# A selective-scan kernel: in each POOL step, the due inflows ahead of the C product of the last chunk

## What is computed

```python
def _ssm(u, Wdbc, Wdt, bdt, Alog, Dp):          # u: (batch, time, 1024)
    dlt, Bm, Cm = split(einsum('bse,re->bsr', u, Wdbc))
    delta = softplus(einsum('bsr,er->bse', dlt, Wdt) + bdt)
    dA = exp(delta[..., None] * -exp(Alog))      # 16 states n
    dBu = delta[..., None] * Bm[:, :, None, :] * u[..., None]
    h_t = dA_t * h_(t-1) + dBu_t                 # a scan over time, per state
    y_t = einsum('ben,bn->be', h_t, C_t)         # sum over the 16 states
    return y + u * Dp
act_mx = silu(einsum('bsd,ed->bse', x_ssm, Wx) + bx)
out = einsum('bse,de->bsd', act_mx * (z1 + z2), Wf) + bf + skip   # z1 forward, z2 backward
return x + gate * out
```

## Time and profile before

| | |
|---|---|
| median of three runs | 3446.78 us |
| range of the three | 3441.18 to 3452.31 us |
| the profiled execution: its time, its span | 3441.2 us, 3439.6 us |
| VectorE (DVE) busy | 3141.1 us, 91% of the span |
| POOL busy | 3134.4 us, 91% |
| TensorE (PE) busy | 2896.7 us, 84% |
| ScalarE (ACT) busy | 2628.9 us, 76% |
| mean granted TensorE clock | 0.933 of full speed |
| unit 20, an mx unit, from its first scan to the next unit's | 1249.35 to 1296.41, 47.1 us |

### The profile page before, as it was taken

One profiled execution on the slowest core, in us unless ns is written; L12 is line 12 of the kernel. 1 busy time (PEld: TensorE's weight loads), 2 busy tenths in 40 slices (PEclk: granted clock), 3 DMA queues, 4 the chain that ended last, 5 costly groups with the idle time before them and its releaser, 6 DMA issues.

```text
span 3439.6 us, 47915 instructions
## 1 busy us (share of the span) xinstructions
PE 2896.7 (84%) x16208; PEld 2088.2 (61%) x16208; DVE 3141.1 (91%) x2117; ACT 2628.9 (76%) x5032; POOL 3134.4 (91%) x1418
## 2 busy tenths in 40 slices
PE   8997788887778888888889888888889888888888
PEld 4654565666656665566666665666666665666665
DVE  1865999999999999999999999999999999999994
ACT  0225899887887899887777899987777898987772
POOL 0534999999999999999999999999999999999996
PEclk9998999999889999999999999999999999998999
DMA  5566443654456444644557344645557444644553
GB/s 208 199 219 230 148 154 132 221 194 160 148 193 245 133 154 158 246 152 165 186 196 258 131 157 152 250 151 165 182 202 255 131 160 152 246 154 163 183 194 120
DMA packets 224041, 623.12 MB, mean 181 GB/s; under 512 B 21980, under 2 KB 68252, under 8 KB 219960
## 3 DMA queue, kind: packets, MB, share of 16 engines
q1 hardware_dynamic: 221064, 599.11, 50.2%
q0 software_dynamic: 2592, 18.88, 1.6%
q10 hardware_dynamic: 144, 2.10, 0.2%
HBM read 539.75 MB, written 80.24 MB: 180 GB/s over the span
## 4 chain that ended last, share of the span: by engine, by line
POOL 33%; issue 23%; PE 21%; DVE 13%; ACT 1%; DMA 0%; POOLq 0%; DVEq 0%; SPq 0%; ACTq 0%
POOL dbu L1075 17%; POOL hbuf L1080 15%; DVE hbuf L1179 7%; PE y L797 7%; PE mb L770 6%; DVE slot L1179 4%; PE slot L808 3%; PE mb L844 1%; DVE du L1130 1%; PE mb L847 1%; DVE delta L1120 1%; PE mb L880 1%; PE slot L880 0%; PE y L880 0%; POOL skip L1086 0%
## 5 line engine op out<-in xcount | busy, mean ns | idle before, releaser
L1080 POOL TENSOR_TENSOR hbuf<-hbuf,cres 128x1024 f32<-128x1024 f32 x640 | 1508.1, 2373 | 33.6 <-DVE hbuf L1179 32.6
L1075 POOL TENSOR_TENSOR dbu<-bst,du 128x1024 f32<-128x1024 f32 x640 | 1506.9, 2373 | 34.5 <-DVE du L1130 22.5
L797 PE MATMUL y<-ident,hbuf 128*128 128x128 f32 x8192 | 1129.0, 289 | 295.3 <-POOL hbuf L1080 292.1
L797 PEld LDWEIGHTS y<-ident,hbuf 128*128 128x128 f32 x8192 | 997.2, 149 | 486.2 <-POOL hbuf L1080 384.7
L1001 ACT ACTIVATE abuf<-dut,bt 128x128 f32<-128x128 f32 x3072 | 971.0, 387 | 0.0
L1179 DVE TENSOR_TENSOR_SCAN hbuf<-dec,slot 128x1024 f32<-128x1024 f32 x384 | 874.6, 2278 | 41.8 <-PE slot L808 23.7
L1179 DVE TENSOR_TENSOR_SCAN slot<-slot,dbu 128x1024 f32<-128x1024 f32 x384 | 875.6, 2280 | 10.7 <-ACT slot L1039 5.3
L1039 ACT ACTIVATE slot<-delta,par 128x1024 f32<-128x1024 f32 x640 | 710.3, 1110 | 211.9 <-DVE hbuf L1184 198.5
L1179 DVE TENSOR_TENSOR_SCAN hbuf<-slot,dbu 128x1024 f32<-128x1024 f32 x256 | 580.5, 2268 | 1.7 <-ACT slot L1039 1.7
L808 PE MATMUL slot<-ident,abuf 128*128 128x128 f32 x3072 | 424.5, 283 | 178.7 <-ACT abuf L1001 170.7
L1039 ACT ACTIVATE dec<-delta,par 128x1024 f32<-128x1024 f32 x384 | 438.2, 1141 | 156.7 <-DVE hbuf L1179 156.7
(11 more groups left out here) (140 smaller groups left out, 2142.7 us busy)
## 6 DMA issues: line engine op xcount, KB each, us to landing
bst<-bc_s SPq DMA_DIRECT2D x640, 512.0 KB, 4.2
cres<-bc_s SPq DMA_DIRECT2D x128, 512.0 KB, 8.2
wzs<-wz_s SPq DMA_DIRECT2D x64, 256.0 KB
yf_s<-yrd SPq DMA_DIRECT2D x32, 512.0 KB, 5.4
ybuf<-yf_s SPq DMA_DIRECT2D x32, 512.0 KB, 5.8
yg_s<-ybuf SPq DMA_DIRECT2D x31, 512.0 KB, 2.9
si_s<-silu SPq DMA_DIRECT2D x28, 512.0 KB, 6.0
silu<-si_s SPq DMA_DIRECT2D x28, 512.0 KB, 4.5
```

The costliest lines, as they stand in the source:

```text
L797: last = nc.tensor.matmul(y[:, j * P:(j + 1) * P], hbuf[:, q % HR, j * P:(j + 1) * P], ident[:], start=False, stop=(q % N == N - 1), is_tr ...
L1075: nc.gpsimd.tensor_tensor(dbu[:, i % DR, :], bst[:, i % BR, :], du[:, k % 2, :], ALU.mult).then_inc(pool_b, 1)
L1080: nc.gpsimd.tensor_tensor(hbuf[:, q % HR, :], hbuf[:, q % HR, :], cres[:, q % N, :], ALU.mult).then_inc(pool_prod, 1)
```

## The change

```diff
             for k in range(NU):
                 for c in range(N):
                     q = N * k + c
+                    for i in INFLOWS_AT[q]:
+                        inflow(i)
                     if q >= 1 and kind(q - 1) != "V":
                         product(q - 1)
-                    for i in INFLOWS_AT[q]:
-                        inflow(i)
                     if c == 3 and k > 0 and projection_of(k - 1) is not None:
                         finish_result(projection_of(k - 1))
```

## The result

| | before | after |
|---|---|---|
| median of four runs each on one chip | 3449.55 us | 3506.82 us |
| lowest to highest | 3441.18 to 3455.54 | 3495.47 to 3518.60 |
| profiled execution, its span | 3441.2, 3439.6 | 3511.82, 3510.2 |
| mean granted clock in it | 0.933 | 0.939 |

The ratio is 1.0172, with a 95% interval of 1.0146 to 1.0198: the change costs 59 us, 50 to 68. The forecast was 3512.5 us in a range of 3470 to 3565, and slower.

What follows compares the result with a forecast made beforehand. VectorE and POOL, both 91% busy without slack, were taken as the bound. Terms 41.6 + 22.1 - 10 + 12 = 65.7 us, added to a median of 3446.8, gave 3512.5 us, range 3470 to 3565.

Steps and rivals of the forecast that it cites:

- TensorE's new wait: Step 14, mx units: TensorE waits about 2.45 us for the later product of chunk 13 before its sum.
- stall, 32 mx boundaries: Behind step 14 of mx units: VectorE starts the next unit's scan 2 1.3 us later, 32 times, 41.6 us.
- low clock: TensorE behind its wait in mx boundaries: clock falls in 13 of 32, 1.7 us each, 22.1 us.
- absorbed: VectorE's waits for TensorE's turned inflow swallow part of the stall: -10 us, between 0 and 23.7.
- gating units: Step 14, 30 boundaries: POOL's earlier inflow waits 0.4 us for `du`, delaying the next scan 2; 12 us.
- steps 2 and 8: Products of chunks 1 and 7 go behind inflows of chunks 5 and 13; claimed to cost nothing.
- The walk: Step 14, mx units: late product 13 delays its sum, last Wx part, sigmoid, decay and scan 2, by 1.3 us.
- The strict reading: TensorE's clock drops only after an idle monitor window, so short waits cost no clock; the 22.1 us would go.
- rival A: Full clock: TensorE's new wait never costs the clock; +43.6 us, 3490.4 us, chance 0.27.
- Rival C: Absorbed: the stall at scan 2 replaces later waits of VectorE and ScalarE; about +5 us, 3452 us, chance 0.08.
- the wait of L797 at the sum of chunk 13: Sign on TensorE: its wait for POOL moves here from the sum of chunk 14, about 2.4 us in mx units.
- The new waits of L976: Sign on ScalarE: the sigmoid waits about 1.8 us for the last Wx part, some 60 us over 32 boundaries.

Runs made afterwards that it cites:

- the kernel with the decay first: The changed kernel, with ScalarE's decay of chunk 2 put ahead of the second sigmoid half; 3510.10 us, 1.0202.
- one inflow ahead: The kernel before, with only the first of step 14's two inflows ahead of the product of chunk 13; 3456.86 us, 1.0036.
- product 4 ahead: The kernel before, with the product of chunk 4 put ahead of the inflow of chunk 9; 3438.82 us, 0.9980.
- the same with Wf later: The kernel before, product of chunk 4 ahead of inflow of chunk 9, and unit 8's Wf load moved from step 0 to 3; 3429.41 us, 0.9958.
- gating units alone: The kernel before, with the product of chunk 4 ahead of the inflow of chunk 9 only in gating units; 3445.54 us, 0.9997.
- steps 2 and 8 alone: The kernel before, with inflows put ahead of the product in steps 2 and 8 only, step 14 in the old order; 3459.33 us, 1.0022.

## Why the prediction was right

Times of unit 20 are taken from the start of its scan 0 (1249.35 before, 1275.41 after).

| step of the prediction | predicted | measured |
|---|---|---|
| product 13 starts | -1.31 | -1.34 |
| TensorE's new wait | 2.45 us | 2.28 us |
| last Wx part ends | +3.85 | +3.87 |
| sigmoid starts | +3.90 | +3.91 |
| decay ends | +7.56 | +7.59 |
| scan 2 starts | +7.62 | +7.62 |
| stall, 32 mx boundaries | 41.6 us | 42.6 us (32 x 1.33) |
| low clock | 13 x 1.7 = 22.1 us | 11 boundaries, 16.5 us |
| absorbed | -10 us | -5.9 us |
| gating units | 12 us | 8.1 us |
| steps 2 and 8 | 0 | about 3 us at most, within the rows above |
| sum | 65.7 us | 61.3 us by the trace, 59 by the runs |

**The walk.** It held link by link, because every duration was at hand in the trace before and only one start was new. One link was missed: VectorE's silu waits for the sigmoid (0.88 us in unit 20) ahead of scan 2's wait for the decay. The sum does not change, as the decay ends last; but the kernel with the decay first shows that this link alone would keep the stall.

**The clock.** The count came from 10 low stretches of 32 behind a wait of 2.05 us; behind one of 2.28 us it was 11 (10 to 12 in the four kernels that have it), fewer than the 13 taken. In these, scan 2 is later than in the other 21 by another 1.3 to 1.7 us each, 16.5 us in all; the term was 5.6 us too large. The strict reading of the Trainium skill (TensorE: Matmul & The Clock Gate, The HAM clock gate), rival A, would have no such boundary. The 11 speak against it as a rule for waits this short; that the other 21 stayed at full clock behind the same wait shows that the wait's length alone does not decide.

**Absorbed.** 5.9 us, inside the 0 to 23.7 given; it is what is left over (42.6 + 16.5 less the 53.2 of the table), not read from a wait. That nearly all of the stall is paid fits a POOL without slack: its waits ahead of products rose by 48.7 us, nearly the 53.2 us of the mx boundaries.

**Gating units.** The wait for `du` came as forecast, 29 of some 0.4 us beside the one of 22 us at the start. That projecting units lose less goes with `gate_y`, whose wait fell from 43.1 to 19.9 us: the forecast had named this wait as cover, and did not see that it would shrink. No run takes this link by itself; with one inflow ahead, where the wait rose by 10.3 us, the projecting boundaries lost 12.5 us.

**The sum.** That it came within 5 us of the trace is in part luck: the clock's term was 5.6 us too large and the gating term 3.9, what is absorbed was taken 4.1 us too high, and the stall was 1 us too small. Rival C's sum does not come out: 53.6 less 41.8 leaves 11.8 us, not 5, and that is outside the 10 us it was to stay within.

**The signs.** Most came true: the wait of L797 at the sum of chunk 13 (2.3 us), the 48.40 us of unit 20, the waits for `du`. Two had wrong sizes. The new waits of L976 are 74.3 us, not some 60, which is what they would be at full clock; and scan 2 waits 0.25 us for the decay, not 1.3 (0.26 and not 3 at the lower clock), as the silu's wait comes first. One was a poor sign: rival A was to be told by an unchanged mean clock. The mean rose from 0.933 to 0.939 while the low clock cost 16.5 us. And "nothing" for step 2 rested on who waits for the product alone; the experiment shows a second condition, that the inflow ahead finds its B row landed. It is met in the full change only because step 14 moves as well.

## What to carry to other kernels

When two operations on a full in-order engine change places, follow the one that comes later into the queue of its consumer, and look at what stands there behind it: here the same late product cost nothing or 1.3 us each time, by whether one group of matmuls stood ahead of the wait or behind it. Such a price has a threshold (one place later 0 us, two places 53 us), so reorder on the waiting engine as well before giving up a swap. And check the operation that comes earlier too: its data must be asked for earlier, not only its turn.

## What the runs showed of the hardware

**A short wait, either clock.** Behind waits of 2.28 and 2.29 us of TensorE the granted clock was 1.00 in one boundary and 0.50 in another. There were 11 low ones in 32 of the changed kernel, and 10, 12 and 12 in the three other kernels with this wait; in the rest none was seen, though the count goes by a late scan 2 and would miss a low clock that nobody waits for. What decides it is open.

**The set-up part has two levels.** It is the same code in all kernels, and up to scan 12 of unit 0 it took 334.7 to 339.7 us in eight of the profiles and 343.4 to 351.5 us in the others. One window of it, in the kernel before:

```profile
160.00:180.00 20.00, 20.00 (x91) 11.85 (x90) 18.60 (x36) 6.58 (x10) 9.12 (x8) 1.00 0.80 255
```

and in the changed kernel:

```profile
160.00:180.00 20.00, 20.00 (x81) 11.12 (x80) 18.60 (x37) 5.71 (x9) 9.11 (x8) 0.91 0.67 214
```

TensorE is busy throughout in both, and the clock is 0.91 in one. That is a mean: in windows of 2 us it is 1.00 but for short falls some 17 us apart (0.50 at 140, 174 and 208 us, 0.57 and 0.55 at 156 and 192), and no matmul between 140 and 240 us has a wait of over 0.05 us ahead of it. Eight matmuls of one product (L378) take 5.35 us from 172.72, against 3.65 us in the kernel before. Between 136 and 236 us the six profiles with the long set-up have three to six such falls, the eight others none to three. In windows of 20 us from 140 to 240 us the clock was 0.91 in four of the changed kernel and 0.85 in the other, against 0.99 to 1.00 in the kernel before. The runs of one kernel fall into two groups some 12 us apart in the same way: many of the kernel before are near 3441 or near 3452.5 us. Read group by group, the small differences agree with the table, which leaves the set-up out: product 4 ahead 3427 and 3439 (-14, table -14.4), the same with Wf later about 3428.5 and 3441.5 (-12, table -11.8), gating units alone about 3431 and 3445.5 (-7 to -10, table -9.8), steps 2 and 8 alone 3463 (+10, table +10.4). So the medians of 0.9980, 0.9958 and 0.9997 differ mostly by how many runs fell into which group. For the executions without a profile this is inferred from the two groups, not shown; what sets the level is open.
